# Grouped attention of a decoder on one Trainium2 core: the output product moved behind the second projection, the banks of the fills in another order, the last step of the quantising moved to GpSimd

## The chip, the core and the metric

One core of a Trainium2 chip runs the whole program. The metric is the device time of one execution in microseconds (us); three executions of the kernel before give a median. A separate execution is recorded by the hardware profiler. The engines are TensorE (PE; its weight loads are listed as PEld), VectorE (DVE), ScalarE (ACT), GpSimd (POOL) and SyncE (SP), which here issues the transfers.

## The reference, cut to what matters

The program is a decoder of six residual layers over x of shape 4 x 256 x 256. The change lies in the fifth, `_L1_xattn_ref`, attention with 16 heads of width 128 in 8 groups of 2:

```
ln_out = _ln(hidden_states, ln_w, ln_b)
q  = _ln(_fp8_linear_pertensor(ln_out, wq, ...));   k = _ln(... wk ...);   v = ... wv ...
core = _gqa(q, k, v)                       # softmax(q k^T / sqrt(d)) v, per group and sequence
qx = _ln(... wqx ...);  kx, vx = split(cond @ w_kv_x);  kx = _ln(kx)
xout = _gqa(qx, kx, vx)
cat  = concatenate([core, xout])
catq = _div_clamp_fp8(cat, proj_smooth)    # clip to +-448, round to bfloat16, then to the fp8 grid
out  = einsum('bsi,oi->bso', catq, wproj) * (proj_in_scale * proj_w_scale)
```

The result is added to x. The rounding to the fp8 grid is done by arithmetic on bfloat16 values y: e is the exponent part of y, bounded below by 2^-6 and multiplied by 24; then (y + e) - e is y rounded.

## The kernel before

The grouped attention is cut into 32 items (8 groups times 4 sequences) and runs as a software pipeline of 36 slots. In slot n (class `Slot`) the engines work on five items at once: the projections of item n (`projects`), the scores of item n-1 (`scores`), the normalising and transposing of the probabilities of item n-2 (`turns`), the average of the values of item n-3 (`averages`), and the quantising, output product and residual addition of item n-4 (`outputs`). The remainder s = n mod 4 says which weights of the next group are prepared in the slot (`next_weights`); for s = 3 DVE has no part in that, and for n from 29 on there is none.

The order of the work is written by hand, one function `visit(o)` for each engine. Before, it is:

- PE: `project_item(o, 0)`, `next_weights`, `output_item`, `project_item(o, 1)`, `turn_item_heads`, `average_item`, `score_item`.
- DVE: `invert_sums(0)` (L1501), `quantise_item` (L1489, then `round_steps`, L196 to L199), `invert_sums(1)`, `next_weights` (L1462, L1467), `lay_item_probs(0)` (four scalings L1507, one transposition L1513), `add_item` (L1520), `lay_item_probs(1)`, `normalise_item` (L1482), `item_max` (L1496).
- ACT: `next_weights` (L1097 to L1105), `take_projection` (L1118, L1120), `take_item_heads` (L1127, L1134), `take_item_average` (L1149, which writes `cat_y`), `softmax_item` (L1161).
- POOL: `head_scale(o, 0)` and `head_scale(o, 1)` (L1691, L1692: twelve values in all, which `normalise_item` waits for).
- SP: in slots with s = 3 the loads of a later group's weights, in slots with s = 0 those of the output weights; then `move_item_probs`: 16 transfers (L554) that carry the transposed blocks from `probs_laid` to `probsT`.

`average_item` of the next slot waits for those 16 transfers, and so does the first transposition of the next slot's `lay_item_probs`, which writes the same `probs_laid`.

PSUM has 8 banks. Banks 0 to 3 hold the projections. The other results, called fills, share banks 4 to 7: two fills of weights, one of the output product (ADD), three of turned heads (HEADS_T), two of averages (OUT) and four of scores (SCORES), twelve in a slot. `FILL_BANKS` gives the bank of each, `plan_slot` their order. PE claims a bank when every fill planned in it earlier has been read out (`claim`, `drained`). So who has to read a bank out before PE can go on follows from this list:

```
WEIGHTS, ADD, HEADS_T, OUT, SCORES = 0, 2, 3, 6, 8
FILL_BANKS = (5, 6, 4, 7, 4, 5, 6, 7, 4, 5, 6, 7)
```

An older part of the kernel, before slot 0 and between slots 1 and 2, quantises the attention's input in a similar way: DVE's L1445, L1448, L1449 and L1450 (`quantise`), with the last subtraction on POOL (`split`, L1704, the same shapes and types as L199).

Of the kernel before, what the change touches and what calls it, by code (L numbers as in the profile page):

```python
# [25 lines left out]
U16 = mybir.dt.uint16  # L26
U32 = mybir.dt.uint32
ALU = mybir.AluOpType
# [162 lines left out]

def round_steps(v, order, y, e, out):

    order.link(v.tensor_scalar(e.bitcast(U16), y.bitcast(U16), 0x7F80, None, ALU.bitwise_and))  # L196
    order.link(v.tensor_scalar(e, e, 2.0 ** -6, 24.0, ALU.max, ALU.mult))
    order.link(v.tensor_tensor(y, y, e, ALU.add))
    return v.tensor_tensor(out, y, e, ALU.subtract)  # L199


class Fills:


# [47 lines left out]


WEIGHTS, ADD, HEADS_T, OUT, SCORES = 0, 2, 3, 6, 8
FILL_BANKS = (5, 6, 4, 7, 4, 5, 6, 7, 4, 5, 6, 7)
W_FILLS = 6
ITEMS = G * B
FIRST_STEPS = {8: (0, 1), 9: (2, 3), 11: (4, 5)}
# [25 lines left out]
def slot_weights(o):  # L284

    if o.s == 0:
        return o.g, (6, 7)
    return o.g + 1, (2 * o.s - 2, 2 * o.s - 1)


def plan_slot(f, o):


    def fill(*fills_of):
        for j in fills_of:
            f.plan(FILL_BANKS[j], ("slot", o.n, j))

    if o.projects:
        f.plan(0, ("proj", o.n, 0))
        f.plan(1, ("proj", o.n, 1))  # L300
    if o.n == 0:
        f.plan(4, ("Yc", 1, 0))
        f.plan(5, ("Yc", 1, 1))
    if o.weights:
        fill(WEIGHTS, WEIGHTS + 1)
    if o.outputs:
        fill(ADD)
    if o.projects:
        f.plan(2, ("proj", o.n, 2))
        f.plan(3, ("proj", o.n, 3))  # L310
    if o.scores:
        fill(*range(HEADS_T, HEADS_T + 3))
    if o.n == 1:
        f.plan(5, ("xT", "Q", 1, 0))
        f.plan(6, ("xT", "Q", 1, 1))
    if o.averages:
        fill(OUT, OUT + 1)
    if o.scores:
        fill(*range(SCORES, SCORES + 4))
# [93 lines left out]
def front_stage(nc, c, a):  # L413

    with Stage(nc) as st:
        fills = Fills(st.sem, 8)
# [22 lines left out]
        raw_p_loaded = st.sem("raw_p_loaded")  # L439
        proj_read, rstd_ready, negated = st.sem("proj_read"), st.sem("rstd_ready"), st.sem("negated")  # L440
        probs_laid = st.sem("probs_laid")
        probs_moved, cat_ready = [st.sem(f"probs_moved{par}") for par in both], st.sem("cat_ready")

        base = (0, 18)
        x = [c.x_all[:, h] for h in both]
        xn, xT = c.xn, c.xT
# [59 lines left out]
        with nc.Block() as block:  # L506
# [76 lines left out]
            def _(pe):  # L583
# [201 lines left out]
                def heads_out(h):  # L785
                    fills.wait_drained(pe, ("O", 4 * h + 3))
                    project("Yc", h, oT[h], c.w_outT)
# [22 lines left out]
                def next_weights(o):  # L810
                    if o.s == 0:
                        pe.wait_ge(raw_p_loaded, (o.g + 1) * (16 * P_LOADS))
                    if o.s == 1:
                        pe.wait_ge(raw_loaded, (o.g + 2) * (16 * LOADS))
                    g, ws = slot_weights(o)
                    for i, w in enumerate(ws):
                        turn_weight(("slot", o.n, WEIGHTS + i), w)
# [92 lines left out]
                def visit(o):  # L910
                    if o.projects:
                        project_item(o, 0)
                    if o.n == 0:
                        heads_out(1)
                    if o.weights:
                        next_weights(o)
                    if o.outputs:
                        output_item(o)
                    if o.projects:
                        project_item(o, 1)  # L920
                    if o.scores:
                        turn_item_heads(o)
                    if o.n == 1:
                        turn_tokens("Q", 1, twice[1], normed_count("Q2"))
                    if o.averages:
                        average_item(o)
                    if o.scores:
                        score_item(o)
# [322 lines left out]
            def _(v):  # L1251
                order = Order(v, dve_order)
# [233 lines left out]
                def quantise_item(o):  # L1486
                    for side in range(2):
                        fills.wait_drained(v, ("slot", o.n - 1, OUT + side))
                    order.link(v.tensor_scalar(c.cat_y, c.cat_y, FP8_MAX, -FP8_MAX, ALU.min, ALU.max))  # L1489
                    round_steps(v, order, c.cat_y, c.cat_e, c.cat.rearrange("p i n -> p (i n)")).then_inc(cat_ready, 1)  # L1490

                def item_max(o, side):
                    for h in range(HPG):
# [5 lines left out]
                def invert_sums(o, side):  # L1499
                    fills.wait_drained(v, ("slot", o.n - 1, SCORES + 2 * side + 1))  # L1500
                    order.mark(v.reciprocal(c.score_inv[:, 4 * side:4 * side + 4], c.score_sum[:, 4 * side:4 * side + 4]))  # L1501

                def lay_item_probs(o, side):
                    order.wait()
                    for i in range(4):
                        p = c.probs[:, side, i // 2, i % 2, :]
                        order.mark(v.tensor_scalar(p, p, c.score_inv[:, 4 * side + i:4 * side + i + 1], None, ALU.mult))  # L1507
                    order.wait()
                    before = o.n - 3
                    if side == 0 and before >= 0:  # L1510
                        v.wait_ge(probs_moved[before % 2], (before // 2 + 1) * (16 * MOVES))
                    laid = c.probs_laid.rearrange("p k j (s i b) -> p s i (k j) b", s=2, i=4)[:, side]
                    v.transpose(laid, c.probs[:, side].rearrange("p h t (k b) -> p (h t) k b", b=32)).then_inc(probs_laid, 1)  # L1513
# [8 lines left out]
                def visit(o):  # L1522
                    if o.turns:
                        invert_sums(o, 0)
                    if o.outputs:
                        quantise_item(o)
                    if o.turns:
                        invert_sums(o, 1)
                    if o.weights:
                        next_weights(o)  # L1530
                    if o.turns:
                        lay_item_probs(o, 0)
                    if o.outputs:
                        add_item(o)
                    if o.turns:
                        lay_item_probs(o, 1)
                    if o.projects:
                        normalise_item(o)
                    if o.n == 1:
                        for m in range(len(KINDS)):  # L1540
                            quantise(1, m)
                    if o.scores:
                        item_max(o, 0)
                        item_max(o, 1)
# [93 lines left out]
            def _(pool):  # L1638
                order = Order(pool, pool_order)
# [49 lines left out]
                def head_scale(o, t):  # L1689
# [2 lines left out]
                    pool.tensor_tensor(c.head_rstd[:, t, :], c.head_sum[:, t, :], c.minus_half[:, 0:6],  # L1692
                                       ALU.pow).then_inc(rstd_ready, 1)

                def visit(o):
                    if o.projects:
                        head_scale(o, 0)
                        head_scale(o, 1)
# [377 lines left out]
```

## Time and profile before

| what | value |
|---|---|
| time, median of 3 runs | 1064.17 us (1063.57 to 1068.45) |
| the profiled execution: its own time, its span from first to last instruction | 1067.66 us, 1066.0 us |
| mean granted clock of TensorE | 0.942 |
| PE busy, DVE busy, ACT busy, POOL busy | 86%, 68%, 53%, 14% of the span |
| `quantise_item` first and last starts in | 393.98 us (slot 4), 931.97 us (slot 35) |

The page of the profile gives these. Its times count from the span's start. "q" below is the start of L1489 in a slot, from which the other times of the slot are counted. A timeline row gives start, length, engine, line, operation, what it writes and reads, shapes, how many are merged in the row, and in brackets how long the engine was idle before and what ended that.

### The profile page before, as it was taken

Reading aid. Unit: us, or ns where it says so; the run is one execution under the profiler, and the core shown is the slowest. Engines: PE = TensorE matmul, PEld = TensorE weight load, DVE = VectorE, ACT = ScalarE, POOL = GpSimd, SP = SyncE. Lnnn points to the kernel's source line nnn. Section 1 sums busy time; section 2 is a strip of 40 time slices with the busy share of each in tenths; the row PEclk is TensorE's granted clock in tenths of the full one; section 3 lists DMA queues with packets and bytes.
Section 4 is the critical chain, followed back from the end, with each engine's and each line's share of the span. In section 5 each row is a group of like instructions: output and inputs, shape, how many; then the busy total and the mean of one; then the engine's idle time right before and its main releaser. Section 6 shows DMA issues by size and latency. Waiting matters only on the chain. (4 is left out here: it accounts for less than half of the span.)

```text
span 1066.0 us, 15923 instructions
## 1 busy us (share of the span) xinstructions
PE 920.6 (86%) x5254; PEld 691.2 (65%) x5254; DVE 728.0 (68%) x1575; ACT 566.9 (53%) x2102; POOL 147.2 (14%) x190
## 2 busy tenths in 40 slices
PE   6989896999856589999999999999999987659597
PEld 3657664566545477778787887787877775444354
DVE  4564545567774777878787888787878786446554
ACT  4351333544524577777677777777777665121131
POOL 2001202000033411121212111111111120000000
PEclk9998998999888699999999999999999998769899
DMA  6010000000100042332332423324222522200000
GB/s 203 1 59 1 0 1 1 2 1 1 41 1 20 1 114 73 89 94 68 100 80 56 124 58 101 83 58 109 71 70 55 179 57 68 49 1 1 20 0 20
DMA packets 64081, 56.77 MB, mean 53 GB/s; under 512 B 11201, under 2 KB 62978, under 8 KB 64002
## 3 DMA queue, kind: packets, MB, share of 16 engines
q1 hardware_dynamic: 63904, 55.76, 19.7%
q8 instruction: 41, 0.67, 0.3%
q14 instruction: 38, 0.31, 0.1%
q10 hardware_dynamic: 98, 0.03, 0.0%
HBM read 21.15 MB, written 1.05 MB: 21 GB/s over the span
## 5 line engine op out<-in xcount | busy, mean ns | idle before, releaser
L1161 ACT ACTIVATE group_probs<-ps,score_bias 128x256 f32<-128x256 f32 x256 | 117.4, 484 | 57.0 <-DVE score_bias L1496 57.0
L837 PE MATMUL ps<-group_w_hi,xq 128*128 128x256 f32 (+1 forms) x512 | 131.1, 297 | 18.8 <-POOL xq L1704 11.6
L1118 ACT ACTIVATE group_squares<-ps 128x128 f32<-128x128 f32 x384 | 103.8, 297 | 71.9 <-PE ps L837 61.7
L1496 DVE TENSOR_REDUCE score_bias<-ps 128x2 f32<-128x512 f32 x128 | 88.1, 691 | 67.8 <-PE ps L891 67.8
L837 PE MATMUL ps<-group_w_lo,xq 128*128 128x256 f32 (+1 forms) x512 | 123.9, 283 | 0.0
L878 PE MATMUL ps<-group_probsT,group_values 128*128 128x512 f32 x256 | 117.3, 602 | 2.7 <-issue 2.7
L891 PE MATMUL ps<-group_kT,group_qT 128*128 128x256 f32 x512 | 115.8, 379 | 2.3 <-ACT group_qT L1127 2.3
L891 PEld LDWEIGHTS ps<-group_kT,group_qT 128*128 128x128 f32 x512 | 97.1, 190 | 28.4 <-issue 16.8
L837 PEld LDWEIGHTS ps<-group_w_hi,xq 128*128 128x128 f32 x512 | 100.2, 196 | 21.4 <-DVE group_heads L1482 7.6
L906 PE MATMUL ps<-group_wp_hi,group_cat 128*128 128x256 f32 x256 | 71.3, 312 | 43.0 <-DVE group_cat L199 43.0
L837 PEld LDWEIGHTS ps<-group_w_lo,xq 128*128 128x128 f32 x512 | 100.6, 196 | 0.8
L1513 DVE STREAM_TRANSPOSE second<-group_probs 128x1024 f32<-128x1024 f32 x64 | 79.7, 1245 | 11.8 <-DMA group_probsT<-second 9.9
L906 PEld LDWEIGHTS ps<-group_wp_hi,group_cat 128*128 128x128 f32 x256 | 52.7, 206 | 52.2 <-DVE group_cat L199 52.2
L1118 ACT ACTIVATION_READ_ACCUMULATOR group_squares<-ps 128x1 f32 x384 | 86.3, 228 | 0.0
L1692 POOL TENSOR_TENSOR head_rstd<-head_sum,minus_half 128x6 f32<-128x6 f32 x64 | 84.8, 1325 | 5.3
L878 PEld LDWEIGHTS ps<-group_probsT,group_values 128*128 128x128 f32 x256 | 47.1, 194 | 50.1 <-issue 49.9
L1149 ACT ACTIVATE group_cat_y<-ps,vec_inv 128x256 bf16<-128x256 f32 x128 | 55.2, 496 | 45.1 <-PE ps L878 45.1
L1482 DVE TENSOR_TENSOR group_heads<-ps,head_rstd 128x384 f32<-128x384 f32 x128 | 63.2, 540 | 17.3 <-POOL head_rstd L1692 17.3
L1691 POOL TENSOR_SCALAR head_sum<-head_sum 128x6 f32<-128x6 f32 x64 | 13.8, 215 | 430.4 <-ACT group_values L1120 430.4
L1507 DVE TENSOR_SCALAR group_probs<-group_probs,score_inv 128x256 f32<-128x256 f32 x256 | 72.4, 346 | 0.4
L906 PE MATMUL ps<-group_wp_lo,group_cat 128*128 128x256 f32 x256 | 67.8, 298 | 0.0
L852 PE MATMUL ps<-group_w_x,ctxT 128*128 128x256 f32 x256 | 67.4, 387 | 0.0
(262 smaller groups left out, 1797.9 us busy)
## 6 DMA issues: line engine op xcount, KB each, us to landing
group_probsT<-second SPq DMA_DIRECT2D x512, 64.0 KB, 2.0
group_raw_p<-in_L_xattn_wproj_dram SPq DMA_DIRECT2D x16, 256.0 KB, 3.3
group_raw_w<-in_L_xattn_wq_dram SPq DMA_DIRECT2D x8, 256.0 KB, 3.1
group_raw_w<-in_L_xattn_wqx_dram SPq DMA_DIRECT2D x8, 256.0 KB, 3.1
group_raw_w<-in_L_xattn_w_kv_x_dram SPq DMA_DIRECT2D x16, 128.0 KB, 3.2
x_all<-in_x_dram SPq DMA_DIRECT2D x2, 512.0 KB, 5.9
front_work<-in_ctx_dram SPq DMA_DIRECT2D x1, 1024.0 KB, 6.8
group_raw_w<-in_L_xattn_wk_dram SPq DMA_DIRECT2D x8, 128.0 KB, 3.0
```

Of the source, the lines that this page charges most:

```text
L837: last = pe.matmul(c.ps[:, bank, at:at + width], x_, w[:, k, col:col + width], start=k == 0 and m == 0, stop=k == KD - 1 and m == 1)
L852: last = pe.matmul(c.ps[:, bank, 256:512], c.ctxT[:, b, k, t * P:(t + 1) * P], c.w_x[par][:, k, :], start=k == 0, stop=k == KD - 1)
L878: last = pe.matmul(c.ps[:, bank, :].rearrange("p (i n) -> p i n", i=BLOCKS), c.values[:, o.seq_of_average, kt, side, :], c.probsT[item % 2 ...
L891: last = pe.matmul(c.ps[:, bank, t * S:(t + 1) * S], c.qT[:, side, h, t * P:(t + 1) * P], c.kT[:, side, :], start=True, stop=True)
L906: last = pe.matmul(c.ps[:, bank, t * D:(t + 1) * D], c.cat[:, i, t * P:(t + 1) * P], w[:, i, :], start=i == 0 and m == 0, stop=i == 3 and ...
L1118: act.activation(c.squares[:, t, 3 * i + h, :], c.ps[:, bank, h * HD:(h + 1) * HD], ACT.Square, accum_out=c.head_sum[:, t, 3 * i + h:3 * i ...
L1161: last = act.activation(c.probs[:, side, h, t, :], c.ps[:, fills.bank(name), t * S:(t + 1) * S], ACT.Exp, bias=c.score_bias[:, i:i + 1], a ...
L1482: fills.drain(v.tensor_tensor(c.heads[:, o.par, t, 3 * i:3 * i + 3, :], c.ps[:, fills.bank(name), 0:3 * HD].rearrange("p (h n) -> p h n", ...
L1496: v.tensor_reduce(c.score_bias[:, i:i + 2], c.ps[:, bank, :].rearrange("p (t n) -> p t n", n=S), AX.X, ALU.max, negate=True).then_inc(nega ...
L1507: order.mark(v.tensor_scalar(p, p, c.score_inv[:, 4 * side + i:4 * side + i + 1], None, ALU.mult))
L1513: v.transpose(laid, c.probs[:, side].rearrange("p h t (k b) -> p (h t) k b", b=32)).then_inc(probs_laid, 1)
L1692: pool.tensor_tensor(c.head_rstd[:, t, :], c.head_sum[:, t, :], c.minus_half[:, 0:6], ALU.pow).then_inc(rstd_ready, 1)
```

## The change

It has four parts.

1. PE runs `output_item` behind `project_item(o, 1)`, no longer before it, and `plan_slot` plans the fill ADD at the new place.
2. `FILL_BANKS` becomes a strict rotation 5, 6, 4, 7. So the second and third HEADS_T use banks 5 and 6, behind the two fills of weights; the first OUT uses bank 4, behind ADD; the four SCORES use 5, 6, 4, 7.
3. The last step of the quantising, `cat = cat_y - cat_e`, leaves DVE. POOL does it in a new function `finish_quantise` at the head of its slot, after a new semaphore `cat_rounded`. The first four steps stay on DVE.
4. DVE's order in a slot becomes `invert_sums(0)`, `quantise_item`, `lay_item_probs(0)`, `invert_sums(1)`, `next_weights`, `lay_item_probs(1)`, `add_item`, `normalise_item`, `item_max`.

```diff
--- before.py
+++ after.py
@@ -191,14 +191,6 @@
 
 
 
-def round_steps(v, order, y, e, out):
-
-    order.link(v.tensor_scalar(e.bitcast(U16), y.bitcast(U16), 0x7F80, None, ALU.bitwise_and))
-    order.link(v.tensor_scalar(e, e, 2.0 ** -6, 24.0, ALU.max, ALU.mult))
-    order.link(v.tensor_tensor(y, y, e, ALU.add))
-    return v.tensor_tensor(out, y, e, ALU.subtract)
-
-
 class Fills:
 
 
@@ -252,7 +244,7 @@
 
 
 WEIGHTS, ADD, HEADS_T, OUT, SCORES = 0, 2, 3, 6, 8
-FILL_BANKS = (5, 6, 4, 7, 4, 5, 6, 7, 4, 5, 6, 7)
+FILL_BANKS = (5, 6, 4, 7, 5, 6, 4, 7, 5, 6, 4, 7)
 W_FILLS = 6
 ITEMS = G * B
 FIRST_STEPS = {8: (0, 1), 9: (2, 3), 11: (4, 5)}
@@ -303,16 +295,16 @@
         f.plan(5, ("Yc", 1, 1))
     if o.weights:
         fill(WEIGHTS, WEIGHTS + 1)
-    if o.outputs:
-        fill(ADD)
     if o.projects:
         f.plan(2, ("proj", o.n, 2))
         f.plan(3, ("proj", o.n, 3))
+    if o.outputs:
+        fill(ADD)
     if o.scores:
         fill(*range(HEADS_T, HEADS_T + 3))
     if o.n == 1:
-        f.plan(5, ("xT", "Q", 1, 0))
-        f.plan(6, ("xT", "Q", 1, 1))
+        f.plan(4, ("xT", "Q", 1, 0))
+        f.plan(7, ("xT", "Q", 1, 1))
     if o.averages:
         fill(OUT, OUT + 1)
     if o.scores:
@@ -439,6 +431,7 @@
         raw_p_loaded = st.sem("raw_p_loaded")
         proj_read, rstd_ready, negated = st.sem("proj_read"), st.sem("rstd_ready"), st.sem("negated")
         probs_laid = st.sem("probs_laid")
+        cat_rounded = st.sem("cat_rounded")
         probs_moved, cat_ready = [st.sem(f"probs_moved{par}") for par in both], st.sem("cat_ready")
 
         base = (0, 18)
@@ -914,10 +907,10 @@
                         heads_out(1)
                     if o.weights:
                         next_weights(o)
+                    if o.projects:
+                        project_item(o, 1)
                     if o.outputs:
                         output_item(o)
-                    if o.projects:
-                        project_item(o, 1)
                     if o.scores:
                         turn_item_heads(o)
                     if o.n == 1:
@@ -1487,7 +1480,9 @@
                     for side in range(2):
                         fills.wait_drained(v, ("slot", o.n - 1, OUT + side))
                     order.link(v.tensor_scalar(c.cat_y, c.cat_y, FP8_MAX, -FP8_MAX, ALU.min, ALU.max))
-                    round_steps(v, order, c.cat_y, c.cat_e, c.cat.rearrange("p i n -> p (i n)")).then_inc(cat_ready, 1)
+                    order.link(v.tensor_scalar(c.cat_e.bitcast(U16), c.cat_y.bitcast(U16), 0x7F80, None, ALU.bitwise_and))
+                    order.link(v.tensor_scalar(c.cat_e, c.cat_e, 2.0 ** -6, 24.0, ALU.max, ALU.mult))
+                    v.tensor_tensor(c.cat_y, c.cat_y, c.cat_e, ALU.add).then_inc(cat_rounded, 1)
 
                 def item_max(o, side):
                     for h in range(HPG):
@@ -1525,15 +1520,14 @@
                     if o.outputs:
                         quantise_item(o)
                     if o.turns:
+                        lay_item_probs(o, 0)
                         invert_sums(o, 1)
                     if o.weights:
                         next_weights(o)
                     if o.turns:
-                        lay_item_probs(o, 0)
+                        lay_item_probs(o, 1)
                     if o.outputs:
                         add_item(o)
-                    if o.turns:
-                        lay_item_probs(o, 1)
                     if o.projects:
                         normalise_item(o)
                     if o.n == 1:
@@ -1692,7 +1686,16 @@
                     pool.tensor_tensor(c.head_rstd[:, t, :], c.head_sum[:, t, :], c.minus_half[:, 0:6],
                                        ALU.pow).then_inc(rstd_ready, 1)
 
+                def finish_quantise(o):
+
+                    pool.wait_ge(cat_rounded, o.n - 3)
+                    if o.n > 4:
+                        fills.wait_full(pool, ("slot", o.n - 1, ADD))
+                    pool.tensor_tensor(c.cat.rearrange("p i n -> p (i n)"), c.cat_y, c.cat_e, ALU.subtract).then_inc(cat_ready, 1)
+
                 def visit(o):
+                    if o.outputs:
+                        finish_quantise(o)
                     if o.projects:
                         head_scale(o, 0)
                         head_scale(o, 1)
```

## Rows read from the trace of the kernel before

**Rows 1.** Waits between 395 and 934 us: total us, times, longest us.
```profile
PE ps L906 <- DVE group_cat L199: 38.6, 25, 4.5
...
DVE second L1513 <- DMA group_probsT<-second: 6.9, 7, 2.2
```

**Rows 2.** Timeline of DVE in slot 18 (s = 2).
```profile
640.84 0.41 DVE L1489 TENSOR_SCALAR group_cat_y<-group_cat_y 128x1024 bf16<-128x1024 bf16 x1
...
642.21 0.69 DVE L198 TENSOR_TENSOR group_cat_y<-group_cat_y,group_cat_e 128x1024 bf16<-128x1024 bf16 x1
...
644.17 1.10 DVE L1462 SCALAR_TENSOR_TENSOR group_w_lo<-ps,w_scale,group_w_hi 128x128 fp32r<-128x128 f32 x4
645.18 1.13 DVE L1507 TENSOR_SCALAR group_probs<-group_probs,score_inv 128x256 f32<-128x256 f32 x4
646.34 1.25 DVE L1513 STREAM_TRANSPOSE second<-group_probs 128x1024 f32<-128x1024 f32 x1
647.51 0.65 DVE L1520 TENSOR_TENSOR x_all<-x_all,ps 128x512 f32<-128x512 f32 x1
```

**Rows 3.** Timeline of PE in slot 18: first output product, second projection, average.
```profile
644.22 0.39 PE L906 MATMUL ps<-group_wp_hi,group_cat 128*128 128x256 f32 x1 [1.10 <-DVE group_cat L199]
...
646.23 0.28 PE L837 MATMUL ps<-group_w_hi,xq 128*128 128x256 f32 x1
...
648.93 1.47 PE L865 MATMUL ps<-ident,group_heads 128*128 128x128 f32 x12
650.24 3.60 PE L878 MATMUL ps<-group_probsT,group_values 128*128 128x512 f32 x8
```

**Rows 4.** Timeline of DVE: weights in slots 4 and 5, first and last regular q.
```profile
397.31 1.38 DVE L1467 SCALAR_TENSOR_TENSOR group_wp_lo<-ps,out_scale,group_wp_hi 128x512 fp32r<-128x512 f32 x2
...
412.60 0.41 DVE L1489 TENSOR_SCALAR group_cat_y<-group_cat_y 128x1024 bf16<-128x1024 bf16 x1
...
416.01 1.77 DVE L1462 SCALAR_TENSOR_TENSOR group_w_lo<-ps,w_scale,group_w_hi 128x256 fp32r<-128x256 f32 x4
...
816.37 0.41 DVE L1489 TENSOR_SCALAR group_cat_y<-group_cat_y 128x1024 bf16<-128x1024 bf16 x1
```

**Rows 5.** Timeline of all engines, 348.9 to 352.1 us, in the older quantising.
```profile
348.70 0.69 DVE L1450 TENSOR_TENSOR front_work<-front_work 128x1024 bf16<-128x1024 bf16 x1
349.31 0.42 DVE L1445 TENSOR_SCALAR front_work<-front_work 128x1024 bf16<-128x1024 bf16 x1
349.48 2.23 POOL L1704 TENSOR_TENSOR xq<-front_work 128x1024 fp32r<-128x1024 bf16 x1 [6.43 <-DVE front_work L1450]
349.77 2.22 DVE L1448 TENSOR_SCALAR front_work<-front_work 128x1024 uint16<-128x1024 uint16 x1
...
352.02 0.43 DVE L1449 TENSOR_SCALAR front_work<-front_work 128x1024 bf16<-128x1024 bf16 x1
```

**Rows 6.** The line L1448: ns min/median/max, first and last start us.
```profile
L1448 DVE TENSOR_SCALAR front_work<-front_work x8: 427/2219/2221, 291.7 to 357.4; 128x1024 uint16<-128x1024 uint16 x8
```

**Rows 7.** Groups by line and shape, 560 to 960 us: busy us, mean ns | idle before.
```profile
L1507 DVE TENSOR_SCALAR group_probs<-group_probs,score_inv 128x256 f32<-128x256 f32 x164 | 46.4, 346 | 0.3
...
L199 DVE TENSOR_TENSOR group_cat<-group_cat_y,group_cat_e 128x1024 fp32r<-128x1024 bf16 x22 | 26.9, 1224 | 0.7
...
L1501 DVE RECIPROCAL score_inv<-score_sum 128x4 f32<-128x4 f32 x40 | 7.0, 174 | 5.5 <-ACT group_probs L1161 5.5
```

**Rows 8.** Timeline of all engines, 750.4 to 752.3 us, a slot with s = 0.
```profile
750.77 1.13 DVE L1507 TENSOR_SCALAR group_probs<-group_probs,score_inv 128x256 f32<-128x256 f32 x4
...
751.47 0.23 POOL L1691 TENSOR_SCALAR head_sum<-head_sum 128x6 f32<-128x6 f32 x1 [11.84 <-ACT group_values L1120]
```

**Rows 9.** Timeline of PE in slot 4.
```profile
403.52 1.09 PE L865 MATMUL ps<-ident,group_heads 128*128 128x128 f32 x8 [0.84 <-DVE x_all L1520]
```

**Rows 10.** Timeline of SP, the transfers of slot 19.
```profile
667.24 10.91 SPq L554 DMA_DIRECT2D group_probsT<-second  x16
```

**Rows 11.** Transfers by line: how many, KB each, median us from issue to landing.
```profile
group_probsT<-second SPq DMA_DIRECT2D x512, 64.0 KB, 2.0
```

**Rows 12.** Timeline of PE in slot 33: its average.
```profile
910.74 4.14 PE L878 MATMUL ps<-group_probsT,group_values 128*128 128x512 f32 x8
```

**Rows 13.** Two stretches: us, busy us of PE, PEld, DVE, ACT, POOL; then PEclk, DMA.
```profile
340.00:352.00 12.00, 5.38 (x32) 4.44 (x31) 6.58 (x10) 7.87 (x21) 4.92 (x4) 1.00 0.00 0
348.00:356.00 8.00, 1.73 (x8) 1.20 (x7) 7.76 (x10) 2.31 (x4) 4.49 (x2) 0.75 0.00 0
```

## The prediction

> **What bounds the kernel now.** I read four views in this order: the waits, the timelines of DVE and PE for one slot, the timeline of the older quantising (because a part of the change does there already what it will now do here), and the stretches with the granted clock.
>
> The waits name the target of the change: PE stands 38.6 us in 25 waits before `output_item` because `cat` comes late from DVE [rows 1]. The slot's timelines show why. In slot 18, q is 640.84; `cat` is ready and PE starts the output product at 644.22, q+3.38, after 1.10 us of idleness. Then PE runs without another wait: second projection from 646.23, turned heads from 648.93, average from 650.24, which is q+9.40, then the scores [rows 2, 3]. The scores give the maxima, the exponentials and the sums from which the next q follows. So one loop closes per slot: DVE's quantising (3.38) and PE's chain behind it. It has the same length whatever weights the slot prepares: from the q of slot 5 to that of slot 28 are 816.37 - 412.60 = 403.77 us, 23 slots of 17.555 us [rows 4]. From the start of the average to the next q are 17.55 - 9.40 = 8.15 us. DVE's laying of probabilities lies beside this loop today and ends nothing in it.
>
> **The change part by part.** The total is made against the profiled execution (span 1066.0, its own time 1067.66, 1.7 outside the span); the median of the runs is 1064.2, and I put the difference on that.
>
> *PE's order.* Nothing is added or removed; the wait of 1.10 goes if `cat` is there when the second projection is done. That projection takes 648.93 - 646.23 = 2.70 [rows 3], so PE wants `cat` at 3.38 - 1.10 + 2.70 = q+4.98, and would be ready for the average at 9.40 - 1.10 = q+8.30. If nothing else moved, a slot would take 16.45.
>
> *The last step on POOL.* L199 (1224 ns, 22 times in the group [rows 7]) leaves DVE. POOL has done the same subtraction on the same shapes: L1704 starts 0.78 after the start of the addition before it (348.70 to 349.48) and takes 2.23 [rows 5]. The addition L198 starts at q+1.37 [rows 2], so POOL starts at q+2.15 and `cat` is ready at q+4.38. That is 0.6 before PE wants it; the cover is the second projection, and without it (slots 32 to 35) `cat` is 4.38 - 3.32 = 1.06 late. POOL's own `head_scale` is queued behind it, but its inputs come later (the one at 751.47 had found POOL idle for 11.84 us [rows 8]), so it costs nothing.
>
> *What that step does to DVE.* This is the term that decides. In the older quantising DVE goes on with L1445, already started, and then issues L1448 at 349.77 while POOL's subtraction runs. L1448 then takes 2.22 instead of 0.43 and ends at 351.99, 0.28 after POOL's end (349.48 + 2.23 = 351.71) [rows 5]. It is not one case: of 8 executions the shortest is 427 ns and the median 2219 [rows 6]. So a fast SBUF-to-SBUF scaling of DVE stands still while that subtraction runs. In the new order exactly such operations follow at once: the four L1507 of `lay_item_probs(0)`. Are they of the blocked sort? They are fast: a tiny operation takes 174 ns (L1501), and L199 needs 1224 for 1024 elements, so 1.03 ns an element; at that pace 256 elements would take some 440, and L1507 takes 346 [rows 7]. And they do meet POOL: in the train that began at 750.77 the third L1507 ended near 751.64, and L1691, issued at 751.47, was not done before 751.70, a little after it, with the fourth L1507 already issued [rows 8]. So POOL gets its turn between two of a train, it isn't kept out to the train's end. The Trainium skill says the same as a rule ("SBUF — State Buffer", section "Who interferes with whom"): `tensor_scalar` in a 2-port mode and GpSimd share a port pair, the first to issue holds it for the whole instruction and the other fully blocks. By that rule the sum is the one below; it speaks against this change, and the trace agrees with 2.22 against 0.43 us.
>
> So, from rows: the train starts 0.61 after L198 (as L1445 after L1450 [rows 5]), at q+1.98. The first L1507 passes, POOL then holds DVE off until q+4.38, the second ends 0.20 after that (0.28 less the 0.08 by which L1507 is shorter than L1448), two more follow 0.26 apart ((1.13 - 0.35)/3 [rows 2]), and the transposition starts at q+5.1. Unblocked it would start at 1.98 + 1.16 = q+3.14. The bounds are these two: 0 and 2.0 us a slot. I take 2.0, as L1448 is the nearest row.
>
> *DVE's order and the banks together.* The first OUT now takes bank 4, behind ADD, so PE may not start the average before `add_item` has read ADD. `add_item` now stands behind both transpositions and the weights. Today a similar claim (second HEADS_T in bank 4 behind ADD) is nearly always free; in slot 4 it does bite, 0.84 us [rows 9]. In the new order, from the start of the first transposition: 1.17 to the next operation, 0.1 for `invert_sums(1)`, the weights, 1.16 for four scalings, 1.17 for the second transposition, 0.65 for the addition [rows 2] = 4.25 plus weights. The weights are 0 for s = 3, 645.18 - 644.17 = 1.01 for s = 2, 1.30 for s = 0 and 1.69 for s = 1 (their lengths less the 0.08 of overlap [rows 4]). With 5.1 in front and 0.05 for the claim, the average starts at q+9.40, 10.41, 10.70 and 11.09 for s = 3, 2, 0, 1, always after the 8.30 at which PE is ready. Adding 8.15, the slots take 17.55, 18.56, 18.85 and 19.24, four together 74.20 against 70.22. With 6 rounds of four (slots 5 to 28): 6 x 3.98 = +23.9.
>
> The other new claims (HEADS_T in banks 5 and 6 behind the weights) cost nothing: DVE has read the weights by 5.1 + 1.27 + 1.69 = q+8.1 at worst, and heads that wait for it end before 11.09. SP's transfers start with the end of the second transposition; 16 are issued in 10.91 and the last lands 2.0 after its issue, so some 12.3 [rows 10, 11]. With slots this long they land before q+4 of the next slot, ahead of both waits for them.
>
> *The ends.* Slots 29 to 31 have no weights: 17.55 as before, 0. Slot 4 has a late transfer in front of the new, longer way to `add_item`: up to +2.8; slot 2's transfers start some 2 earlier, since its laying no longer stands behind its weights: I take +1, bounds -1 and +3. In slots 32 to 35 there is no second projection: `cat` is 1.06 late twice on the path (32, 35), and in slot 33 the average, now at q+6.96 [rows 12], waits for `add_item` at q+9.4, +2.4; slot 34 may give 0.9 back. I take +4, bounds +2 and +6.
>
> Sum: 23.9 + 0 + 1 + 4 = +29. That makes the span 1095 and the median 1093 us, +2.7%.
>
> **The rivals.**
>
> *DVE isn't blocked (ends faster).* If L1507 doesn't contend with POOL, or POOL's share is short as with L1691's few elements, the first transposition is ready at q+3.14. Then the transfers decide a little: they land some 12.3 after the second transposition's end, about q+3.5. The average starts at 8.30, 8.81, 9.10 and 9.49, four slots take 68.3, 6 x -1.9 = -11.5; slots 29 to 31 give 4, the ends cost 4: -11.5, so 1053. Note how small the gain is even so: most of the 1.10 is lost again to `add_item` before the average. For it: none of the rows shows L1507 against a long POOL operation. Against it: [rows 5 to 8]. It decides when the block is under some 1.0 us a slot: with the transposition at q+4.1 the average starts at 8.4, 9.4, 9.7 and 10.1, and four slots take 70.2 again.
>
> *POOL is kept out until the train's end.* If back-to-back L1507s hold their turn, the train ends at q+3.1, `cat` is ready near q+5.3, 0.3 after PE wants it, and DVE loses nothing: the average starts no earlier than 8.6, four slots take 68.6: -10, the rest +2: 1056. Against it: L1691 in [rows 8].
>
> *The clock falls on top.* PE now stands for 1.1 to 2.8 us in one piece before the average. In 340 to 352 us PE was busy for 5.38 of 12 us and the granted clock stayed at 1.00 (2.4 GHz); in 348 to 356, busy for 1.73 of 8, it was 0.75, half of the stretch at 1.2 GHz [rows 13]. The idle pieces here are nearer to the first stretch, so I take no fall. Should it fall in the slots with s = 1 and s = 0, average and scores (7.05 us) lose up to 3.4 in each: 12 slots x 2.5 = +30, 1123; with s = 1 alone about 1108.
>
> *It does nothing.* The wait of 1.10 goes and 1.1 comes back elsewhere: that would take a block of about 1.0, between the bounds, for which no row speaks.
>
> **How the numbers follow.** The blocked case without a fall of the clock: 0.62, 1093, its own range 1084 to 1106 (a slot more or less by 0.4, and the ends' bounds). With a fall: 0.18, 1106 to 1125. Unblocked: 0.10, 1053. POOL kept out: 0.05, 1056. About nothing: 0.05, 1060 to 1069. The range 1076 to 1120 leaves out the last three and the far end of the second. A change of 0.5% (5 us) is about what a measurement of this kernel can tell from none: faster 0.13, same 0.06, slower 0.81.
>
> **What the profile will show.** Right: in every slot one or two L1507 of the first train take about 2.2 us instead of 0.35; the new POOL subtraction takes 2.2 to 2.3; the wait of L906 for `cat` is gone; PE's L878 waits for L1520 by 1.1 to 2.8 us; slots differ with s, longest for s = 1. Wrong: if L1507 stays at 346 ns, the block fails and the slots fall to 16.5 to 17.6; if L906 waits for POOL, the subtraction is longer than in the older quantising; if L878 doesn't wait for L1520, the bank's claim is not where I put it; if PEclk falls below 1.00 between 411 and 829 us, the clock rival is at work.

## The result: 3.0% slower, and the profile after

The changed kernel takes 1097.69 us (median of 4 runs, 1096.7 to 1100.38) against 1066.1 (4 runs of the kernel before, 1063.57 to 1068.45): ratio 1.030, 95% interval 1.027 to 1.033. The profiled execution has its own time 1097.82 and a span of 1096.2 us; before they were 1067.66 and 1066.0. So the profile shows 30.2 us more, where the prediction's sum had 29; the median is 4.7 us above the forecast 1093.

The waits between 395 and 960 us of the kernel after show the exchange (columns as in [rows 1]):

```profile
PE ps L871 <- DVE x_all L1515: 54.0, 30, 2.3
...
PE ps L899 <- POOL group_cat L1694: 16.2, 3, 5.4
```

PE's wait for `cat` is gone but for three waits in the slots without a second projection (a fourth, in slot 35, lies behind this window). In its place PE waits in 30 slots before the average (L871) for the residual addition (L1515): 54.0 us.

Why the addition is late is seen on DVE in slot 18, which answers to [rows 2]; q is 655.96:

```profile
655.96 0.41 DVE L1482 TENSOR_SCALAR group_cat_y<-group_cat_y 128x1024 bf16<-128x1024 bf16 x1
...
657.33 0.69 DVE L1485 TENSOR_TENSOR group_cat_y<-group_cat_y,group_cat_e 128x1024 bf16<-128x1024 bf16 x1
657.94 3.02 DVE L1502 TENSOR_SCALAR group_probs<-group_probs,score_inv 128x256 f32<-128x256 f32 x4
660.99 1.25 DVE L1508 STREAM_TRANSPOSE second<-group_probs 128x1024 f32<-128x1024 f32 x1
662.16 0.14 DVE L1496 RECIPROCAL score_inv<-score_sum 128x4 f32<-128x4 f32 x1
662.22 1.09 DVE L1455 SCALAR_TENSOR_TENSOR group_w_lo<-ps,w_scale,group_w_hi 128x128 fp32r<-128x128 f32 x4
663.22 1.13 DVE L1502 TENSOR_SCALAR group_probs<-group_probs,score_inv 128x256 f32<-128x256 f32 x4
664.39 1.25 DVE L1508 STREAM_TRANSPOSE second<-group_probs 128x1024 f32<-128x1024 f32 x1
665.56 0.65 DVE L1515 TENSOR_TENSOR x_all<-x_all,ps 128x512 f32<-128x512 f32 x1
```

The first train of four scalings takes 3.02 us, the second 1.13. GpSimd's timeline of the same slot has what lies beside the first:

```profile
658.10 2.18 POOL L1694 TENSOR_TENSOR group_cat<-group_cat_y,group_cat_e 128x1024 fp32r<-128x1024 bf16 x1 [11.42 <-DVE group_cat_y L1485]
```

and the line of the scalings (ns min/median/max, as in [rows 6]) shows that such a scaling can take 2.23 us instead of 0.35; in each of slots 4 to 33 it is the second of the first train:

```profile
L1502 DVE TENSOR_SCALAR group_probs<-group_probs,score_inv x256: 338/346/2233, 359.3 to 940.4; 128x256 f32<-128x256 f32 x128
```

PE's timeline of that slot closes the argument; it answers to [rows 3]:

```profile
662.67 1.48 PE L858 MATMUL ps<-ident,group_heads 128*128 128x128 f32 x12
666.35 1.96 PE L871 MATMUL ps<-group_probsT,group_values 128*128 128x512 f32 x4 [2.20 <-DVE x_all L1515]
```

The addition ends at 665.56 + 0.65 = 666.21, q+10.25, and the average starts at 666.35, q+10.39. PE had been idle for 2.20 us by then. Before, the average started at q+9.40.

The starts of L1482, the q of slots 13 to 17 (s = 1, 2, 3, 0, 1), answer to [rows 4]:

```profile
562.40 0.42 DVE L1482 TENSOR_SCALAR group_cat_y<-group_cat_y 128x1024 bf16<-128x1024 bf16 x1
...
581.55 0.41 DVE L1482 TENSOR_SCALAR group_cat_y<-group_cat_y 128x1024 bf16<-128x1024 bf16 x1
...
600.17 0.42 DVE L1482 TENSOR_SCALAR group_cat_y<-group_cat_y 128x1024 bf16<-128x1024 bf16 x1
...
617.92 0.41 DVE L1482 TENSOR_SCALAR group_cat_y<-group_cat_y 128x1024 bf16<-128x1024 bf16 x1
...
636.81 0.41 DVE L1482 TENSOR_SCALAR group_cat_y<-group_cat_y 128x1024 bf16<-128x1024 bf16 x1
```

The slots are no longer equal: 19.15, 18.62, 17.75 and 18.89 us, four together 74.41. Forecast were 19.24, 18.56, 17.55 and 18.85, together 74.20.

Two stretches of the kernel after (columns as in [rows 13]) show the main thing that the sum left out. The first holds slot 12, which lasted 20.60 us, the second slot 13:

```profile
541.00:563.00 22.00, 19.73 (x115) 15.83 (x114) 16.18 (x31) 14.23 (x62) 5.23 (x5) 0.92 0.33 86
562.00:582.00 20.00, 18.37 (x117) 15.63 (x117) 15.88 (x32) 14.10 (x61) 5.37 (x5) 1.00 0.19 46
```

In slots 4, 12 and 20 TensorE's granted clock fell from 2.4 to 1.2 GHz for a part of the slot, each time within 0.7 us of the end of PE's idle piece before the average (2.3 us). Slot 12 was 20.60 - 18.90 = 1.7 us longer than slot 8 of the same s.

### The profile page after: what moved, and what is told of

Read it like the earlier page. It is cut to its first block and busy times, and to the rows that moved or that the text cites. A ratio compares the mean times of both kernels' runs of the same rounds, so it can differ in the third digit from the quotient of the medians.

```text
span 1096.2 us, 15954 instructions
## 1 busy us (share of the span) xinstructions
PE 921.3 (84%) x5254; PEld 691.4 (63%) x5254; DVE 742.2 (68%) x1543; ACT 566.4 (52%) x2102; POOL 217.9 (20%) x222
## 5 line engine op out<-in xcount | busy, mean ns | idle before, releaser
L871 PE MATMUL ps<-group_probsT,group_values 128*128 128x512 f32 x256 | 122.4, 623 | 54.0 <-DVE x_all L1515 54.0
L1694 POOL TENSOR_TENSOR group_cat<-group_cat_y,group_cat_e 128x1024 fp32r<-128x1024 bf16 x32 | 69.5, 2172 | 385.9 <-DVE group_cat_y L1485 385.9
L1502 DVE TENSOR_SCALAR group_probs<-group_probs,score_inv 128x256 f32<-128x256 f32 x256 | 129.0, 566 | 0.5
L884 PE MATMUL ps<-group_kT,group_qT 128*128 128x256 f32 x512 | 118.8, 386 | 4.3 <-ACT group_qT L1120 4.3
L871 PEld LDWEIGHTS ps<-group_probsT,group_values 128*128 128x128 f32 x256 | 47.8, 197 | 109.6 <-issue 109.3
L1111 ACT ACTIVATE group_squares<-ps 128x128 f32<-128x128 f32 x384 | 109.2, 343 | 11.5 <-PE ps L830 10.9
L1111 ACT ACTIVATION_READ_ACCUMULATOR group_squares<-ps 128x1 f32 x384 | 98.4, 276 | 0.0
L899 PE MATMUL ps<-group_wp_hi,group_cat 128*128 128x256 f32 x256 | 73.6, 321 | 21.7 <-POOL group_cat L1694 21.5
```

Of the source, the lines that this page charges most:

```text
L871: last = pe.matmul(c.ps[:, bank, :].rearrange("p (i n) -> p i n", i=BLOCKS), c.values[:, o.seq_of_average, kt, side, :], c.probsT[item % 2 ...
L884: last = pe.matmul(c.ps[:, bank, t * S:(t + 1) * S], c.qT[:, side, h, t * P:(t + 1) * P], c.kT[:, side, :], start=True, stop=True)
L899: last = pe.matmul(c.ps[:, bank, t * D:(t + 1) * D], c.cat[:, i, t * P:(t + 1) * P], w[:, i, :], start=i == 0 and m == 0, stop=i == 3 and ...
L1111: act.activation(c.squares[:, t, 3 * i + h, :], c.ps[:, bank, h * HD:(h + 1) * HD], ACT.Square, accum_out=c.head_sum[:, t, 3 * i + h:3 * i ...
L1694: pool.tensor_tensor(c.cat.rearrange("p i n -> p (i n)"), c.cat_y, c.cat_e, ALU.subtract).then_inc(cat_ready, 1)
```

## The experiments

All times are medians in us; each ratio is against the kernel before on the same chip in the same runs (1063.5 to 1064.1). Lines are numbered by each kernel's own file, so L1502, L1503 and L1510 below are the same scalings.

**1. The last step back on DVE.** From the changed kernel:

```diff
-                    v.tensor_tensor(c.cat_y, c.cat_y, c.cat_e, ALU.add).then_inc(cat_rounded, 1)
+                    order.link(v.tensor_tensor(c.cat_y, c.cat_y, c.cat_e, ALU.add))
+                    v.tensor_tensor(c.cat.rearrange("p i n -> p (i n)"), c.cat_y, c.cat_e, ALU.subtract).then_inc(cat_ready, 1)
```

(`finish_quantise` and its call go.)

> The changed kernel with the last subtraction back on DVE; new PE order, new banks and new DVE order stay. Theory (GpSimd's subtraction blocks DVE's scalings for some 2 us, and the average waits for the residual addition behind them): the four L1507 return to 0.35 us each, but stand behind 1.14 us of subtraction on DVE, so the first transposition starts at q+4.4 and not 5.03; every slot from 5 to 31 is 0.6 shorter, total 1075 to 1081 against 1098. Rival (the new order and banks alone cost the time, the blocking is hidden): the 1.14 us come on top on DVE, 1098 or up to 1129.

Measured: 1075.68 (1073.24 to 1076.46), ratio 1.010, interval 1.008 to 1.013. Every L1502 is short again, though 1.14 us of subtraction now stand in front of them:

```profile
L1502 DVE TENSOR_SCALAR group_probs<-group_probs,score_inv 128x256 f32<-128x256 f32 x256 | 72.7, 348 | 0.5
```

The transposition starts at q+4.41 (5.03 in the changed kernel), and PE still waits for the addition. So GpSimd's step costs 22 us here: 0.62 us in each of the 27 slots from 5 to 31, which makes 17, and some 5 because without it the clock stays at 2.4 GHz through slots 4 to 31. The other 12 us over the kernel before are what the new orders of PE and DVE and the new banks cost together.

**2. Only the last step on GpSimd**, PE's order, banks and DVE's order as before:

```diff
-round_steps(v, order, c.cat_y, c.cat_e, c.cat...).then_inc(cat_ready, 1)
+(the first three steps as they are)
+v.tensor_tensor(c.cat_y, c.cat_y, c.cat_e, ALU.add).then_inc(cat_rounded, 1)
...
+                    if o.outputs:
+                        finish_quantise(o)
```

> The kernel before with only the last subtraction moved to GpSimd; PE order, banks and DVE order as before. Theory: cat is ready at q+4.3 and not 3.32, and PE waits for it directly, so each slot is 1.0 us longer (17.55 to 18.5) and the end some 3 us: about 1097. L1507 is stretched only where it meets the subtraction, off the path. Rival (DVE relieved of 1.22 us a slot gains): 1066 or less.

Measured: 1122.40 (1118.79 to 1129.11), ratio 1.054, interval 1.049 to 1.059. The direction was right and the size was not. The waits between 395 and 960 us:

```profile
PE ps L907 <- POOL group_cat L1703: 56.5, 29, 5.4
```

PE now waits for GpSimd, and ten slots last 18.5 as expected. The other 18 of slots 4 to 31 last 20.0. Two stretches (columns as in [rows 13]), a long slot and a short one:

```profile
606.00:626.00 20.00, 17.96 (x100) 15.13 (x100) 14.07 (x27) 12.22 (x55) 5.24 (x5) 0.91 0.41 110
...
646.00:664.50 18.50, 17.57 (x110) 14.80 (x110) 13.76 (x31) 13.28 (x57) 5.17 (x5) 1.00 0.21 50
```

In all 18 long ones, and in none of the short ones, the granted clock falls to 1.2 GHz for a while. 18 x 1.5 = 27 us are the clock's, about as many as the later `cat` costs (28 x 0.95 = 27).

**3. Only PE's order**, with the old banks:

```diff
-                    if o.outputs:
-                        output_item(o)
                     if o.projects:
                         project_item(o, 1)
+                    if o.outputs:
+                        output_item(o)
```

(and the same exchange in `plan_slot`.)

> The kernel before with only the output product moved behind the second projection; old banks (second turned heads behind ADD), old DVE order, subtraction on DVE. Theory: the wait for cat goes, but the second turned heads wait some 0.3 to 0.5 us for the residual addition, which itself must wait for the later product; slots 16.85 to 17.9, mean 17.15, total about 1055 (1050 to 1060). Rival (PE's place of the product doesn't matter, as DVE's chain decides): 1064 to 1068.

Measured: 1052.87 (1049.1 to 1057.32), ratio 0.988, interval 0.984 to 0.992. The waits between 395 and 880 us show what is left:

```profile
PE ps L865 <- DVE x_all L1520: 16.2, 28, 2.7
```

**4. Other banks under the whole change**, so that the averages don't stand behind the addition (all twelve fills get other banks by it, and so do two that only slot 1 has):

```diff
-FILL_BANKS = (5, 6, 4, 7, 5, 6, 4, 7, 5, 6, 4, 7)
+FILL_BANKS = (0, 1, 2, 3, 0, 1, 3, 0, 1, 2, 3, 0)
+RING = (5, 6, 4, 7)
...
-            f.plan(FILL_BANKS[j], ("slot", o.n, j))
+            f.plan(RING[(FILL_BANKS[j] + o.n) % 4], ("slot", o.n, j))
```

> The changed kernel with another assignment of banks 4 to 7 that turns by one from slot to slot, so that the averages no longer stand behind the residual addition; the subtraction stays on GpSimd and the DVE order stays. Theory: L1507 is still blocked (one of 2.2 us in each slot) but PE no longer waits for it; what is left is PE's own work (16.4 to 17.5 us a slot) or the loop of the transfers (4.6 from the first transposition to the end of the second, 12.2 for the transfers: 16.85 in the mean): total 1050 to 1056. Rival (the blocked DVE delays the scores through another way than this bank): stays at 1085 to 1098.

Measured: 1050.21 (1045.86 to 1051.48), ratio 0.987, interval 0.984 to 0.989. The block is still there in full, as the scalings' line shows:

```profile
L1503 DVE TENSOR_SCALAR group_probs<-group_probs,score_inv x256: 337/348/2239, 361.2 to 892.6; 128x256 f32<-128x256 f32 x128
```

but PE no longer waits for the residual addition. 47 us are gained with the same blocking. So nearly all that the late addition costs goes through one path: transposition, addition, bank 4, average. It isn't the only one. What takes over are the transfers, and PE's turned heads now wait in seven places for DVE's weights, which stand behind the held train; the waits between 395 and 860 us:

```profile
DVE second L1509 <- DMA group_probsT<-second: 18.9, 24, 1.7
...
PE ps L859 <- DVE group_wp_lo L1461: 1.9, 3, 1.0
PE ps L859 <- DVE group_w_lo L1456: 1.6, 4, 0.7
```

How much of the 9 us between this run and experiment 5 the block still costs is not shown, since experiment 5 changes DVE's order too.

**5. The best guess of that moment**: experiment 4's banks, the subtraction on DVE, DVE's weights ahead of both layings, the addition last.

```diff
                     if o.turns:
-                        lay_item_probs(o, 0)
                         invert_sums(o, 1)
                     if o.weights:
                         next_weights(o)
                     if o.turns:
+                        lay_item_probs(o, 0)
                         lay_item_probs(o, 1)
```

> All that the experiments so far speak for: product behind the second projection, the banks that turn by one per slot, the last subtraction on DVE, DVE's weights again ahead of both layings, the residual addition behind them. Theory: no engine waits for cat, for the addition or for the transfers (3.7 + 12.2 = 15.9 us a round of that loop), so PE's own work sets the slots: 16.5, 16.7, 17.6, 16.5, and 15.8 for slots 29 to 31; total 1038 to 1043. Rival (DVE with 1.14 us more in its row falls behind the scores): no better than the 1050 of the rotating banks with the step on GpSimd.

Measured: 1041.00 (1038.84 to 1041.7), ratio 0.977, interval 0.974 to 0.979. Slots 19 to 22 (s = 3, 0, 1, 2) are 16.49, 16.74, 17.63 and 16.49.

**6. Half of the step on GpSimd.** The changed kernel, with GpSimd's subtraction cut to the first half of the elements from slot 5 on.

```diff
-                    pool.tensor_tensor(c.cat.rearrange("p i n -> p (i n)"), c.cat_y, c.cat_e, ALU.subtract).then_inc(cat_ready, 1)
+                    w = 4 * S if o.n == 4 else 2 * S
+                    pool.tensor_tensor(c.cat.rearrange("p i n -> p (i n)")[:, 0:w], c.cat_y[:, 0:w], c.cat_e[:, 0:w],
+                                       ALU.subtract).then_inc(cat_ready, 1)
```

> The changed kernel, but from slot 5 on GpSimd subtracts only the first half of the elements of cat; the other half keeps slot 4's values, so that the output is not the reference's. Theory (DVE stands for as long as GpSimd's subtraction lasts): the stretched L1507 falls from 2.2 to some 1.2 us, the transposition starts at q+4.0, every slot is 1.0 shorter, and PE's shorter idle pieces let the clock stay up: 1062 to 1070. Rival (a fixed cost of any meeting of the two engines): L1507 stays near 2.2 us, 1095.

Measured: 1066.08 (1063.47 to 1068.7), ratio 1.001, interval 0.999 to 1.003. GpSimd's line, then (a DVE timeline) the train of scalings in slot 18:

```profile
L1695 POOL TENSOR_TENSOR group_cat<-group_cat_y,group_cat_e x32: 1151/1204/2177, 395.1 to 933.8; 128x512 fp32r<-128x512 bf16 x31, 128x1024 fp32r<-128x1024 bf16 x1
```

```profile
645.68 2.05 DVE L1502 TENSOR_SCALAR group_probs<-group_probs,score_inv 128x256 f32<-128x256 f32 x4
```

The subtraction is 0.98 shorter (2.18 to 1.20), and the train 0.97 (3.02 to 2.05). The rival, a fixed cost of a meeting, falls.

**7. DVE's weights first, subtraction on GpSimd.** The same three lines moved as in experiment 5, in the changed kernel.

> The changed kernel with DVE's inverting and weights ahead of both layings, as before; the subtraction stays on GpSimd, the banks stay. Theory: in slots with s = 0, 1, 2 DVE reads weights from PSUM while GpSimd subtracts, and these aren't blocked; the scalings come when the subtraction is done or nearly so (transposition at q+5.2 to 6.3), and the addition then has no weights in front of it: ends at 9.4 to 10.4 and not 9.4 to 10.8, four slots 72.2 against 74.4, total 1080 to 1086. Rival (the weights' operations are blocked like the scalings): no gain, 1098 or more.

Measured: 1077.96 (1076.58 to 1081.06), ratio 1.013, interval 1.010 to 1.016. The median is 2 us below the expected range. The timeline of DVE and GpSimd in a slot with s = 0:

```profile
680.72 2.15 POOL L1694 TENSOR_TENSOR group_cat<-group_cat_y,group_cat_e 128x1024 fp32r<-128x1024 bf16 x1 [11.68 <-DVE group_cat_y L1485]
681.37 1.41 DVE L1460 SCALAR_TENSOR_TENSOR group_wp_lo<-ps,out_scale,group_wp_hi 128x512 fp32r<-128x512 f32 x2 [0.64 <-ACT group_wp_hi L1098]
682.70 1.13 DVE L1502 TENSOR_SCALAR group_probs<-group_probs,score_inv 128x256 f32<-128x256 f32 x4
```

L1460 runs in the middle of the subtraction and takes 1.41 us (1.38 before, L1467 in [rows 4]). So not every DVE operation is held: these, with one operand in PSUM and one in SBUF, go on. PE still waits for the addition; the waits between 395 and 880 us:

```profile
PE ps L871 <- DVE x_all L1515: 34.9, 27, 1.7
```

**8. PE's order and the new fixed banks alone**; DVE's order and its subtraction as before. It is experiment 3 with the new list (and the two fills that only slot 1 has in banks 4 and 7, as in the whole change):

```diff
-FILL_BANKS = (5, 6, 4, 7, 4, 5, 6, 7, 4, 5, 6, 7)
+FILL_BANKS = (5, 6, 4, 7, 5, 6, 4, 7, 5, 6, 4, 7)
```

> The kernel before with two parts of the change alone: the product behind the second projection and the new fixed banks; DVE's order (addition between the layings) and the subtraction as before. Theory: the addition is then done at q+7.5 to 8.7, ahead of the average (q+8.3 to 9.3), so the average in ADD's bank doesn't wait, and the turned heads no longer wait as in the run of the PE order alone: slots near PE's own work, total 1040 to 1047. So the two harmful parts would be GpSimd's step and DVE's order, not the banks. Rival (an average in the bank behind ADD is bad in itself): 1053 or more.

Measured: 1038.38 (1036.65 to 1041.28), ratio 0.976, interval 0.973 to 0.978: 2.4% faster than the kernel before, 5% faster than the changed one, and 1.6 us below the expected range. It is the lowest median of all, but the interval overlaps with that of experiment 5 (0.974 to 0.979), so which of the two is the better is not settled. The waits between 395 and 860 us:

```profile
DVE second L1513 <- DMA group_probsT<-second: 23.6, 21, 2.6
...
PE ps L878 <- DVE x_all L1520: 6.0, 9, 1.5
```

With the addition between the layings it is done before the average wants bank 4, except in nine slots in which the transfers had delayed the first transposition.

**9. DVE's order alone**, on the kernel before.

```diff
                     if o.turns:
+                        lay_item_probs(o, 0)
                         invert_sums(o, 1)
                     if o.weights:
                         next_weights(o)
                     if o.turns:
-                        lay_item_probs(o, 0)
+                        lay_item_probs(o, 1)
                     if o.outputs:
                         add_item(o)
-                    if o.turns:
-                        lay_item_probs(o, 1)
```

> The kernel before with DVE's new order alone (weights between the layings, residual addition behind both); PE order, banks and the subtraction on DVE as before. Theory: here too a fill in ADD's bank, the second turned heads, must wait for the addition, which ends at q+8.7 to 10.2 as in the run with the last step on DVE; the average starts 1.0 behind it, at q+9.7 to 11.2, four slots take some 75 against 70.2: 1095 to 1110, more if the clock falls. Rival (the order costs only together with GpSimd's step): 1064 to 1070.

Measured: 1097.06 (1091.39 to 1099.24), ratio 1.029, interval 1.025 to 1.033, as much as the whole change. The waits between 395 and 960 us:

```profile
PE ps L865 <- DVE x_all L1520: 26.3, 21, 2.2
```

**10. The change without DVE's order**: experiment 8 with the step on GpSimd, as in experiment 2.

> The whole change but for DVE's order: product behind the second projection, new fixed banks, last subtraction on GpSimd; DVE keeps weights ahead of the layings and the addition between them. Theory: cat is there at q+4.3, ahead of the 4.6 at which PE wants it; L1507 is blocked for up to 2.2 us in the slots with s = 3, but the addition needs the product (ready at q+6.8) anyway, so it ends at 7.5 to 8.7 as without GpSimd, and nothing waits: 1037 to 1044, the same as with the subtraction on DVE. Rival (the blocking costs wherever it occurs): 1060 or more.

Measured: 1043.52 (1041.54 to 1044.75), ratio 0.979, interval 0.977 to 0.982. The first scaling is still held where it meets the subtraction: in the slots with s = 3 and from slot 29 on it takes 2.2 us, in the others with s = 2 0.64 (the mean over all 256 is up, from the 346 of [rows 7] to 434; columns as there):

```profile
L1510 DVE TENSOR_SCALAR group_probs<-group_probs,score_inv 128x256 f32<-128x256 f32 x256 | 95.0, 434 | 0.4
```

Yet it costs little, since the addition behind it must wait for the output product or the transfers anyway. The interval overlaps with that of experiment 8, so the 5 us between the two are not settled.

This kernel and that of experiment 7 differ in one exchange alone, `add_item` before or behind the second laying. Here PE hardly waits for the addition; the waits between 395 and 860 us:

```profile
PE ps L879 <- DVE x_all L1523: 3.6, 7, 0.8
```

So that exchange by itself costs 34 us (1043.5 to 1078.0). The other half of DVE's new order, the first laying ahead of the second inverting and the weights, costs 20 more (1078.0 to 1097.7), some 5 of them the clock's. It sends the scalings into the subtraction in every slot; the slots with s = 3, where they met it already in experiment 7, keep their 17.7 us.

## Why the prediction was right, step by step

The direction, the size (29 of 30.2 us) and the mechanism held. That the sum is off by only 1.2 us is luck in part: it had nothing for the clock, which cost 5.1 us in slots 4, 12 and 20, and its ends were too long by about as much.

*The block on DVE* was forecast at 2.0 us with the transposition at q+5.1; it came at q+5.03. It was L1448 of the older quantising, in [rows 5, 6], that gave it. Experiments 1 (no subtraction on GpSimd, no held scaling) and 6 (half of the subtraction, half of the hold) show that it is GpSimd's operation and lasts as long as it does. GpSimd gets its turn after the first scaling of the train, as [rows 8] had suggested: the rival that it would be kept out falls. What the two engines share was not observed, only that the hold follows the length of the operation and spares the operations of experiment 7.

*Its way to the end* was forecast as addition, bank 4, average. Experiment 4 shows it by taking the averages out of ADD's bank: 47 us, with the hold unchanged. The claim took 0.14 us rather than 0.05; times 24 slots that is 2 us, part of which smaller terms took back (the transposition 0.07 earlier in each slot).

*The slots* were right to 0.2 us each, 74.41 for 74.20. Counted from the q of slot 5 to that of slot 29 the change made 449.81 of 421.32, +28.5, against +23.9 in the sum. The difference has two terms: the 0.2 in four slots (6 x 0.2 = 1.2) and the clock in slots 12 and 20 (3.4).

*The clock* is where the prediction was wrong in part: it gave the fall 0.18 and took none. The fall came, but in 2 of 24 slots instead of 12, and so cost 3.4 us there and not 30 (5.1 with slot 4).

*The ends* were forecast at +5 together and gave about +1.7: slot 4 with its earlier q gave 0.7 back (I had +1), though the clock took 1.7 in it, and from slot 29 on the change cost 2.4 and not 4.

*One number was wrong and did no harm*: that PE would be ready for the average at q+8.30 in every slot. In slots with s = 1 it turns 16 blocks of weights, for 1.95 us, and wasn't waiting for `cat` even before; there PE is ready only at q+9.3. So the waits before the average were 1.3 to 2.3 us and not 1.1 to 2.8, and the wait before `cat` was never worth 1.10 us in all slots, as the unblocked rival had it. Experiment 8 has slots of 17.3 for s = 1 and, where the transfers don't delay them, 16.2 for s = 2 and 3.

*Which part does what* the prediction could not tell, since it costed them together. The experiments can. PE's order gives 11 us alone, and with the banks 26. GpSimd's step costs 58 alone, because PE then waits for it. Behind the second projection, which covers `cat`, it costs about 5 with DVE's old order (experiments 8 and 10, not settled against zero) and 22 with the new one. DVE's order costs 33 alone. In the whole change, taking the step out gives 22 back (1075.7), taking DVE's order out 54 (1043.5), and both 59 (1038.4, experiment 8). So DVE's order is the larger part of the loss. The costs don't add: each sits behind a cover that another part brings or takes away.

## What to carry to other kernels

Moving an elementwise step from VectorE to GpSimd is not free of VectorE: look in the trace for a place where the two already run such operations side by side, and read what the VectorE operation behind it took. When a slot of a software pipeline is reordered, follow each shared bank to the instruction that empties it, and keep that instruction early on its engine; here the same residual addition, behind the second laying and no longer before it, turned a gain of 2.1% (experiment 10) into a loss of 1.3% (experiment 7). Try the parts of such a change one at a time before they are put together.

## What the runs showed of the hardware that I had not expected

The granted clock of TensorE can fall on short idle pieces. In experiment 2 PE stood before `cat` for 1.8 to 2.0 us in one piece in the slots with s = 0, 2 and 3, and for 0.9 us in those with s = 1 up to slot 25. The clock fell to 1.2 GHz in 18 of 28 slots, none of them with s = 1, each time within 1.3 us after such a piece, at a price of 1.5 us each. Slot 29 had a piece of 2.7 us and no fall. In the changed kernel the piece was 2.2 to 2.3 us in the slots with s = 0 and 2, and the clock fell in three of them. Slots of equal s had it in some rounds and not in others. What decides between them stays open; the runs show only the cases counted here, and a price of 1.5 to 1.7 us, somewhat less than the idle piece itself (1.8 to 2.3, or 2.7 in slots 30 and 31 of experiment 2).

A held VectorE operation ends soon after GpSimd's: 0.15 to 0.16 us after it in each of the 30 slots of the changed kernel, and 0.15 when the subtraction was halved. GpSimd's own subtraction is slowed only a little by the meeting: 2.18 us in the changed kernel, where it starts during a scaling, and 2.13 to 2.15 in experiment 7, where it starts beside a reciprocal.
